# The last layer's mask product in halves, and the second half's row maxima one step later

## The reference

```python
def attention(q, k, v, mask):
    scores = jnp.einsum('bhqd,bhkd->bhqk', q, k) / jnp.sqrt(jnp.float32(HD))
    scores = scores * mask - 10000.0 * (1.0 - mask)
    probs = jax.nn.softmax(scores, axis=-1)
    return jnp.einsum('bhqk,bhkd->bhqd', probs, v)
ln_out = layernorm(hidden_states, ln1_s, ln1_b)
q, k, v = jnp.split(ln_out @ w_qkv + b_qkv, 3, axis=-1)
x = hidden_states + merge_heads(attention(..., ltor_mask)) @ w_ao + b_ao
ln_out = layernorm(x, ln2_s, ln2_b)
q = ln_out @ w_q + b_q
k, v = jnp.split(encoder_states @ w_kv + b_kv, 2, axis=-1)
x = x + merge_heads(attention(..., cross_mask)) @ w_co + b_co
return x + gelu(layernorm(x, ln3_s, ln3_b) @ w1 + b1) @ w2 + b2
```

## Time and profile before

| | |
|---|---|
| median of 3 runs | 2332.95 us (2326.84 to 2339.91) |
| profiled execution | 2333.35 us, span 2331.6 us, mean granted TensorE clock 0.949 |
| TensorE busy | 2082.6 us (89%) |
| ScalarE busy | 995.9 us (43%) |
| VectorE busy | 944.8 us (41%) |
| GpSimd busy | 658.7 us (28%) |
| first and last mask product (line 1829) | 1850.66 and 2187.98 us |

### The profile page before, as it was taken

One profiled execution on the slowest core, in us unless ns is written; L12 is line 12 of the kernel. 1 busy time (PEld: TensorE's weight loads), 2 busy tenths in 40 slices (PEclk: granted clock), 3 DMA queues, 4 the chain that ended last, 5 costly groups with the idle time before them and its releaser, 6 DMA issues.

```text
span 2331.6 us, 37925 instructions
## 1 busy us (share of the span) xinstructions
PE 2082.6 (89%) x15565; PEld 1649.3 (71%) x15565; DVE 944.8 (41%) x1726; ACT 995.9 (43%) x2601; POOL 658.7 (28%) x768
## 2 busy tenths in 40 slices
PE   7877788887899999999899999999889877878799
PEld 4555566654688888888788888888755555666566
DVE  3433222302454444445454444444311267667510
ACT  3332344351343443434343343434344356666522
POOL 2311212112232231313223132321120156656500
PEclk9987899997999999999999999999989898989899
DMA  4000000001010000000001000000020100000000
GB/s 135 10 6 1 6 1 1 1 1 41 3 44 19 10 28 1 28 1 19 1 19 46 1 28 10 10 1 1 1 83 0 46 1 2 6 1 6 1 19 19
DMA packets 28174, 38.36 MB, mean 16 GB/s; under 512 B 1744, under 2 KB 19808, under 8 KB 28000
## 3 DMA queue, kind: packets, MB, share of 16 engines
q1 hardware_dynamic: 28000, 35.93, 4.8%
HBM read 33.83 MB, written 2.10 MB: 15 GB/s over the span
## 4 chain that ended last, share of the span: by engine, by line
PE 75%; DVE 8%; ACT 8%; issue 3%; POOL 3%; DMA 1%; SPq 0%; DVEq 0%; ACTq 0%; POOLq 0%
PE ps L184 33%; PE ps L2105 6%; PE ps_four L2251 5%; PE ps_four L2271 4%; PE ps_four L2089 4%; PE ps L2089 3%; PE ps_four L2260 2%; ACT l_pt L1472 2%; POOL l_sm L1322 2%; PE ps_four L2019 2%; PE ps L2147 2%; DVE l_sm L1829 2%; PE ps L2281 1%; PE ps L2057 1%; PE ps L2065 1%
## 5 line engine op out<-in xcount | busy, mean ns | idle before, releaser
L1566 ACT ACTIVATE l_prob<-ps_four,l_mx 128x129 f32<-128x129 f32 x512 | 181.3, 367 | 593.5 <-DVE l_mx L1864 593.5
L1356 POOL TENSOR_TENSOR l_prob<-l_prob,l_mx 128x516 f32<-128x516 f32 x128 | 134.1, 1048 | 779.5 <-DVE l_mx L1871 779.5
L184 PE MATMUL ps<-l_hT,l_wq 128*128 128x512 f32 x768 | 210.8, 410 | 6.5 <-DVE l_V L1852 6.5
L184 PE MATMUL ps<-ctxT,l_wk 128*128 128x512 f32 x768 | 214.3, 415 | 0.0
L184 PEld LDWEIGHTS ps<-l_wo,l_ao 128*128 128x128 f32 x1536 | 197.8, 188 | 21.1 <-DVE l_ao L1883 7.0
L184 PE MATMUL ps<-l_wo,l_ao 128*128 128x256 f32 x1536 | 204.9, 283 | 5.5 <-DVE l_ao L1883 5.5
L184 PE MATMUL ps<-l_wv,ctxT 128*128 128x512 f32 x768 | 204.6, 402 | 3.7 <-POOL l_wv L1294 3.4
L1322 POOL TENSOR_TENSOR l_sm<-l_sm,l_mask 128x1024 f32<-128x1024 f32 x64 | 149.9, 2363 | 155.7 <-DVE l_sm L1829 155.7
L184 PEld LDWEIGHTS ps<-l_wv,ctxT 128*128 128x128 f32 x768 | 143.8, 190 | 47.4 <-ACT l_qT L1547 9.0
L1795 DVE TENSOR_TENSOR x_tok<-x_tok,ps 128x512 f32<-128x512 f32 x100 | 64.7, 684 | 274.1 <-PE ps L2105 212.1
L184 PEld LDWEIGHTS ps<-l_hT,l_wq 128*128 128x128 f32 x768 | 135.8, 190 | 30.3 <-issue 7.2
(11 more groups left out here) (230 smaller groups left out, 3797.6 us busy)
## 6 DMA issues: line engine op xcount, KB each, us to landing
l_staging<-in_L_xattn_wv SPq DMA_DIRECT2D x8, 512.0 KB, 3.8
l_staging<-in_L_xattn_wk SPq DMA_DIRECT2D x8, 512.0 KB, 3.9
l_staging<-in_L_xattn_wq SPq DMA_DIRECT2D x8, 512.0 KB, 4.2
l_staging<-in_L_xattn_wo SPq DMA_DIRECT2D x8, 512.0 KB, 3.8
x_tok<-in_x SPq DMA_DIRECT2D x4, 512.0 KB, 7.4
ctx_tok<-in_ctx SPq DMA_DIRECT2D x4, 512.0 KB, 5.8
l_mlp_w<-in_L_xattn_mlp_w SPq DMA_DIRECT2D x2, 1024.0 KB, 8.8
l_w<-in_L_xattn_w_fc SPq DMA_DIRECT2D x2, 1024.0 KB, 6.3
```

The costliest lines, as they stand in the source:

```text
L184: ins = e.matmul(out, a, b, start=start and i == 0, stop=stop and i == 2, skip_group_check=not check)
L1356: e.tensor_tensor(pr[:, :, 0:S + 1], pr[:, :, 0:S + 1], mx[:, 3, :].unsqueeze(2).to_broadcast([P, GB, S + 1]), ALU.mult).then_inc(sem("poo ...
L1566: ins = e.activation(pr.t[:, b, 0:S + 1], banks[b // 2].t[:, (b % 2) * (S + 2):(b % 2) * (S + 2) + S + 1], ACT.Exp, bias=mx[:, 1, b:b + 1] ...
```

## The change

The mask product (line 1829) is made in two instructions of 8 heads; the first has a semaphore of its own, on which GpSimd's first add waits; the banks are freed by the second. The maxima of heads 8 to 15 leave l3_shift and become a stage of their own, l3_shift2, with ScalarE's eight subtractions. In the plan l3_shift2 of unit n-1 stands right behind scores(n), ahead of the first fill of step n, in place of the end of step n-1. Transposes of banks 2 and 3 wait for l3_shift2. The row maxima's buffer is released by ScalarE's part of l3_shift2, and the mask's by GpSimd's second add.

```diff
         def shifted(n):
             kind, g, b = self.units[n]
             pl.slot(mx, "rowmax", n)
             pl.emit("l3_shift", n)
-            pl.free("rowmax", n, by=("act.l3_shift", n))
             if kind == "b" and b == GB - 1:
-                pl.free("mask2", g, by=("dve.l3_shift:b", n))
+                pl.free("mask2", g, by=("pool.l3_scores", n))
+
+        def shifted_too(n):
+
+            pl.emit("l3_shift2", n)
+            pl.free("rowmax", n, by=("act.l3_shift2", n))
...
                 scores(n)
+            if 1 <= n <= N:
+                shifted_too(n - 1)
             fill()
...
-            q.wait_ge(*pl.event(("empty", "four", "l3", n, 0)))
             for i, name in enumerate(("pool.l3_scores:a", "pool.l3_scores")):
+                if i == 0:
+                    q.wait_ge(*pl.done("dve.l3_scores:a", n))
+                else:
+                    q.wait_ge(*pl.event(("empty", "four", "l3", n, 0)))
...
-        def l3_shift(n):
+        def l3_shift2(n):
 
             sm, mx = use["sm", n].t, use["rowmax", n].t
-            q.wait_ge(*pl.done("dve.l3_shift:b", n))
+            q.wait_ge(*pl.done("dve.l3_shift2", n))
             for h in range(8, 16):
                 ins = e.activation(sm[:, h, :], sm[:, h, :], ACT.Identity, bias=mx[:, h:h + 1])
-            ins.then_inc(sem("act.l3_shift"), 1)
+            ins.then_inc(sem("act.l3_shift2"), 1)
...
-            e.tensor_tensor(sm.t[:], bk.t[:].rearrange("p r (x t) -> p (r x) t", t=S),
-                            mask.unsqueeze(1).to_broadcast([P, 16, S]), ALU.mult).then_inc(bk.slot.empty, 1)
+            for i in range(2):
+                heads = bk.t[:, 2 * i:2 * i + 2, :].rearrange("p r (x t) -> p (r x) t", t=S)
+                e.tensor_tensor(sm.t[:, 8 * i:8 * i + 8, :], heads, mask.unsqueeze(1).to_broadcast([P, 8, S]), ALU.mult).then_inc(
+                    sem("dve.l3_scores:a") if i == 0 else bk.slot.empty, 1)
...
+        def l3_shift2(n):
+            sm, mx = use["sm", n].t, use["rowmax", n].t
             q.wait_ge(*pl.done("pool.l3_scores", n))
-            e.tensor_reduce(mx.t[:, 8:16], sm[:, 8:16, :], AX.X, ALU.max, negate=True).then_inc(sem("dve.l3_shift:b"), 1)
+            e.tensor_reduce(mx[:, 8:16], sm[:, 8:16, :], AX.X, ALU.max, negate=True).then_inc(sem("dve.l3_shift2"), 1)
...
-                q.wait_ge(*pl.done("dve.l3_shift:s" if r < 2 else "act.l3_shift", n))
+                q.wait_ge(*pl.done("dve.l3_shift:s" if r < 2 else "act.l3_shift2", n))
```

More of the change, by code:

```diff
@@ L1585, in scalar_program @@
         stages = dict(const=const, l0_project=l0_project, l0_scores=l0_scores, l1_xT=l1_xT, norm_rstd=norm_rstd, norm_xa=norm_xa,
-                      norm_tr=norm_tr, cols=cols, l1_probs=l1_probs, up32=up32, l3_keys=l3_keys, l3_queries=l3_queries, l3_probs=l3_probs, l3_shift=l3_shift, l1_ao=l1_ao, l3_ao=l3_ao,
+                      norm_tr=norm_tr, cols=cols, l1_probs=l1_probs, up32=up32, l3_keys=l3_keys, l3_queries=l3_queries, l3_probs=l3_probs, l3_shift2=l3_shift2, l1_ao=l1_ao, l3_ao=l3_ao,
                       l2_q=l2_q,
@@ L1911, in vector_program @@
                       norm_shift=norm_shift, norm_xn=norm_xn, norm_split=norm_split, x_add=x_add, rows=rows,
-                      l3_const=l3_const, l3_scores=l3_scores, l3_shift=l3_shift, l3_values=l3_values,
+                      l3_const=l3_const, l3_scores=l3_scores, l3_shift=l3_shift, l3_shift2=l3_shift2, l3_values=l3_values,
                       l2_v=l2_v, l2_scores=l2_scores, l2_norm=l2_norm, l2_tr=l2_tr,
```

## The result

The changed kernel takes 2373.8 us in the median of 4 runs (2370.91 to 2378.21); the kernel before, run beside it, now has 2335.5 us over 4 runs. The ratio is 1.017 (95% interval 1.0134 to 1.0207): slower by 1.7%, some 38 to 40 us. In a second round, against other runs of the kernel before, the changed kernel gave 1.0166 (1.0137 to 1.0194). The forecast was 2362 us in a range of 2332 to 2398. The profiled execution took 2375.99 us, 42.6 more than that of before.

What follows compares the result with a forecast made beforehand. Loop A set the 9.20 us floor; after the change Loop B would bind at 10.15 + 0.8 = 10.95 us. Floor steps +30, the 14 others -1, stage's end -1: +28 on 2333, given as 2362 us, range 2332 to 2398.

Steps and rivals of the forecast that it cites:

- Loop A: Last layer's attention, VectorE's loop with GpSimd from one mask product to the next: 9.17 us before, forecast 7.2 after.
- floor step: One of 17 of the 31 product-to-product steps, 9.20 us in the mean before; forecast 10.95, together +30 us.
- Loop B: Loop through the four PSUM banks (scores, product, transposes, exponentials), with slack before; forecast to decide at 10.15 us a step.
- Scores to product: Link of Loop B from the scores' start on TensorE to the next mask product: 1.31 us.
- rival 3: TensorE's clock goes to the lower level in every step: +1.35 us a step, +42 us, 2404 us; chance 0.12.
- Inserted work: Other groups' norms and projections on ScalarE, half of 1.65 us a step exposed in Loop B: 0.8 us.
- The 14 others: Steps of 10.2 to 15.5 us: about half lose 0.6 us each, half gain some 0.8; together -1 us.
- The end of the stage: End of the last layer's attention: last maxima have no product ahead, GpSimd began 1.06 us sooner; -1 us.
- Rival 1: Loop B overlaps more than added up and falls under 9.2 us, kernel faster: 2304 us; chance 0.07.
- Rival 2: The two loops cancel: inserted work costs nothing inside Loop B, all 14 others gain 1: about 2335 us; chance 0.15.
- Rival 4: GpSimd's first add blocks VectorE's second half product until it ends: +2.3 us a step, +71, 2433 us; chance 0.03.

Runs made afterwards that it cites:

- the halves alone: Kernel before with only the mask product in halves, GpSimd's first add waiting for the first half: 2320.7 us, ratio 0.9922.
- the move alone: Changed kernel with the product whole; only second maxima and ScalarE's subtractions one step later: 2375.7 us, ratio 1.0161 to the kernel before.
- The eight additional activations: Eight more ScalarE activations a unit ahead of the subtractions: kernel before with them 2357.7 us (ratio 1.0099), changed kernel with them 2439.6 us (1.0454).
- the maxima between the halves: Changed kernel, but VectorE takes the earlier unit's second maxima between the two halves of the next product: 2342.5 us, ratio 1.001 to the kernel before.
- the second profile of the changed kernel: Changed kernel itself, nothing edited, run again for comparison on another experiment's chip: 2375.2 us, ratio 1.0166 to the kernel before.
- the last version: Kernel before with the product in halves and the second maxima ahead of VectorE's subtraction of the first half: 2309.6 us, ratio 0.9888.

## Why the prediction was right

The mechanism was right, and the sum fell short by some 10 us: +28 forecast, about +40 measured. The term that was too small is the clock's.

- *Loop A falls.* Right as far as it shows. With the move, VectorE's wait for GpSimd's first half fell from 47.8 to 3.3 us. Loop A's 7.2 us can be seen in one step only, the first, where no late maxima hold up the transposes: 7.02. What it gains by the halves alone is 1.05 us a floor step; the 0.07 us for the second instruction shows as 10.95 against 10.88 between the changed kernel and the move alone.
- *Loop B becomes the longer one.* Right, link by link: 2.28, 1.24, 2.35, 0.83 and 2.09 measured against 2.27, 1.24, 2.36, 0.85 and 2.12. The eight additional activations, 23 us in the one kernel and 66 in the other, and the 37 us that the maxima between the halves bring back, show that these links bind. The eight subtractions start 3.52 us behind the product, against 3.5 forecast.
- *Scores to product, 1.31 us.* This term was mis-sized: 2.16 us in the bare step, since the scores run at the lower clock level. The whole step is 10.95 us where I had 10.15; with the clock up it is 10.03. The forecast had left the clock as it was and made its fall rival 3, with +42 us. What came is between: 14 slow groups and 4 half-slow ones in place of 4 and 2, 9.7 us more of score time, and next to nothing in the transposes, for which the rival had 0.43 us a step. The Trainium skill ("TensorE: Matmul & The Clock Gate", on HAM oscillation) says that gaps in TensorE's work put its clock back to half again and again. The trace agrees in direction, with a granted clock of 0.84 for 0.90, but not in every step: 13 of the 31 had all their scores at 1.17 or 1.18 us.
- *Inserted work, 0.8 us a floor step.* Near, and the closeness of the floor's mean is in part luck: 17 floor steps were forecast at 10.95 us and took 11.30. The forecast had composed its 10.95 of 10.15 and 0.8; measured, the bare floor already is 10.95 at the lower clock. The 16 floor steps behind the first lie 0.61 above it in the mean, and the first, 3.9 below it, hides much of that. So the two terms do add, 0.80 for the clock and 0.61 for inserted work and the rest, in those 16 steps; 12 of them had their scores at 2.09 us. How much of the 0.61 ScalarE's inserted work alone makes was not separated.
- *The 14 others, -1.* They came to +5.9 us. The largest are +2.34, +1.89 and +1.71; which of them TensorE's projections and which the clock brought was not separated. The second is not steady: in the other profile of the same kernel it is +0.25.
- *The end of the stage, -1.* -1.5 us; a shift of 2.7 us ahead of the stage was not forecast and is of the size that single executions differ by (in the second profile of the changed kernel the stage starts at 1850.16 us).

Rival 1 falls: no step had its exponentials ahead of the subtractions, and none but the first stayed below 10.8 (10.03 in the second profile). Rival 2 falls: three of the other steps gave back 1.1 to 1.6 us, but the 14 together lost 5.9. Rival 4 falls: the halves last 1.19 to 1.23 us, beside GpSimd's add or not.

## What to carry to other kernels

Moving an instruction one step later in an engine's order can fill that engine's wait, but it also moves everything behind it in the data's chain. Write down every loop of the pipeline with its links before the move: here one loop fell by 2 us, where it could be seen, and the next, through a buffer with one copy, rose from under 9.2 to 10.95. Try the parts of such a change alone; one of the two was worth 0.8%, and the other cost 1.6% and made it worthless. When a loop lengthens by waits of TensorE, price its links at the lower clock level too.

## What the runs showed of the hardware

A VectorE operation with both inputs in SBUF stands still while a GpSimd operation that began before it runs, rather than running slowly. In the kernel before, the subtraction took 1.22 us alone and 2.12 beside GpSimd's second add. In the last version, where it began earlier in a GpSimd operation, it took 2.92:

```profile
2086.23 2.36 POOL L1304 TENSOR_TENSOR x_tok<-x_tok,l_b 128x1024 f32<-128x1024 f32 x1
2086.76 2.92 DVE L1846 TENSOR_TENSOR l_sm<-l_sm,l_mx 128x1024 f32<-128x1024 f32 x1
```

GpSimd ends at 2088.59, and VectorE 1.09 us after it, at 2089.68: near the length of the operation alone. The 2.12 us ones of the kernel before end 1.08 or 1.09 after GpSimd too. An operation of only 4 elements, with two SBUF inputs, took 1.40 us from 1861.82 in the kernel with the halves, and ended 0.02 after GpSimd's first add. It also holds the other way round. GpSimd's product of the output, 0.72 us otherwise, took 1.71 in the kernel before when it began during VectorE's subtraction, and ended 0.58 after it; the subtraction was not lengthened by it. The halves of the product from PSUM and the maxima, with one SBUF input each, took 1.2 us beside GpSimd's add in every step. The Trainium skill ("SBUF — State Buffer", on who interferes with whom) calls it an exclusive lock, which VectorE's operations with two SBUF inputs contend for; the trace agrees.
